# Two attentions: rows of exponentials scaled by VectorE and turned by TensorE as they are, in place of a product with diagonal matrices

## The reference, cut to what matters

```python
scores = jnp.einsum('bhqd,bhkd->bhqk', q, k) * (1.0 / math.sqrt(D))
scores = jnp.where(causal, scores, -jnp.inf)      # L1_ffn only
att = jax.nn.softmax(scores, axis=-1)
y = jnp.einsum('bhqk,bhkd->bhqd', att, v)
y = y.transpose(0, 2, 1, 3).reshape(B, T, C)
return y @ c_proj_w.T
```

## Time and profile before

| | |
|---|---|
| median of three runs | 1833.15 us (1831.13 to 1835.19) |
| profiled execution, its own time | 1833.63 us |
| its span, first to last instruction | 1831.8 us |
| TensorE busy | 1733.0 us, 95% of the span |
| VectorE, ScalarE busy | 623.2 us, 444.4 us |
| mean granted clock of TensorE | 0.985 |

### The profile page before, as it was taken

One profiled execution on the slowest core, in us unless ns is written; L12 is line 12 of the kernel. 1 busy time (PEld: TensorE's weight loads), 2 busy tenths in 40 slices (PEclk: granted clock), 3 DMA queues, 4 the chain that ended last, 5 costly groups with the idle time before them and its releaser, 6 DMA issues.

```text
span 1831.8 us, 27529 instructions
## 1 busy us (share of the span) xinstructions
PE 1733.0 (95%) x12224; PEld 1040.4 (57%) x12224; DVE 623.2 (34%) x1177; ACT 444.4 (24%) x816; POOL 26.8 (1%) x35
## 2 busy tenths in 40 slices
PE   7999999999999999799999988887999999999998
PEld 4675445754476555577654433334675645768664
DVE  4415994049962211543210000002412422133231
ACT  0014883047831110433110000003411010131110
POOL 0000000000000000000000000000001000000000
PEclk9999999999999999899999999999999899999999
DMA  9205986149747877304579999999362164301661
GB/s 379 109 31 171 210 260 243 52 118 218 242 159 282 328 302 303 114 1 155 207 310 387 427 429 429 427 428 428 130 251 103 68 244 193 132 27 52 259 240 64
DMA packets 80750, 408.28 MB, mean 223 GB/s; under 512 B 9768, under 2 KB 50241, under 8 KB 58993
## 3 DMA queue, kind: packets, MB, share of 16 engines
q1 hardware_dynamic: 76112, 402.41, 58.1%
q10 hardware_dynamic: 4512, 4.03, 0.7%
HBM read 400.85 MB, written 5.51 MB: 222 GB/s over the span
## 4 chain that ended last, share of the span: by engine, by line
PE 80%; DMA 13%; DVE 4%; issue 1%; ACT 1%; SPq 0%; POOL 0%; DVEq 0%; ACTq 0%
PE banks L114 78%; DMA weight_ring<-in_L_ffn_c_fc_dram 8%; PE banks L117 2%; DMA weight_ring<-in_L_ffn_c_proj_e_dram 2%; DMA weight_ring<-in_L_gnn_W_in_dram 2%; DVE weight_ring L120 1%; DMA gate_queries<-in_L_gnn_query_rep_dram 1%; DMA node_parts<-gate_node_parts 1%; DVE stat L266 1%; DMA gate_rows<-node_parts 0%; DVE xn_tok L125 0%; DMA ident<-in_c_ident_dram 0%; SPq L154 0%; DVE xT L137 0%; ACT weight_ring L148 0%
## 5 line engine op out<-in xcount | busy, mean ns | idle before, releaser
L114 PE MATMUL banks<-weight_ring,xT 128*128 128x384 f32 x864 | 293.2, 491 | 1.5 <-DVE rgat_xr L137 1.5
L120 DVE TENSOR_TENSOR weight_ring<-weight_ring,gate_queries 128x1024 f32<-128x1024 f32 x192 | 222.7, 1221 | 18.9 <-ACT weight_ring L148 11.3
L114 PEld LDWEIGHTS banks<-weight_ring,xT 128*128 128x128 f32 x864 | 162.6, 191 | 109.0 <-issue 8.7
L148 ACT ACTIVATE weight_ring<-banks 128x1024 f32<-128x1024 f32 x192 | 191.0, 1024 | 44.0 <-PE banks L114 40.8
L114 PE MATMUL banks<-xT,weight_ring 128*128 128x256 f32 x792 | 178.2, 379 | 3.2 <-ACT x_tok L151 3.2
L114 PEld LDWEIGHTS banks<-xT,weight_ring 128*128 128x128 f32 x792 | 149.8, 190 | 27.4 <-issue 3.6
L114 PE MATMUL banks<-weight_ring,r_xd 128*32 128x384 f32 (+1 forms) x2304 | 142.7, 406 | 0.0
L114 PE MATMUL banks<-weight_ring,moe_xdT 128*64 128x384 f32 x720 | 122.0, 489 | 21.4 <-DMA weight_ring<-in_L_ffn_c_fc_dram 20.4
L114 PEld LDWEIGHTS banks<-weight_ring,r_xd 128*32 128x32 f32 x2304 | 76.7, 110 | 63.2 <-issue 54.9
L114 PE MATMUL banks<-gate_rows,selrow 96*128 96x512 bf16 x384 | 107.4, 381 | 2.9 <-ACT weight_ring L148 1.8
L114 PE MATMUL banks<-weight_ring,selrow 128*32 128x256 f32 x1536 | 102.0, 385 | 2.9 <-DVE weight_ring L120 2.7
(11 more groups left out here) (370 smaller groups left out, 1842.7 us busy)
## 6 DMA issues: line engine op xcount, KB each, us to landing
weight_ring<-in_L_ffn_c_fc_dram SPq DMA_DIRECT2D x30, 2304.0 KB, 23.1
weight_ring<-in_L_ffn_c_proj_e_dram SPq DMA_DIRECT2D x21, 2304.0 KB, 28.3
gate_queries<-in_L_gnn_query_rep_dram SPq DMA_DIRECT2D x48, 512.0 KB, 4.6
weight_slot_heads<-in_L_ffn_c_proj_e_dram SPq DMA_DIRECT2D x9, 2304.0 KB, 28.8
weight_ring<-in_L_ffn_w_gate_dram SPq DMA_DIRECT2D x8, 2304.0 KB, 9.8
weight_ring<-in_L_ffn_w_up_dram SPq DMA_DIRECT2D x8, 2304.0 KB, 8.9
weight_ring<-in_L_ffn_w_down_dram SPq DMA_DIRECT2D x8, 2304.0 KB, 9.6
weight_ring<-in_L_ffn_w_dram SPq DMA_DIRECT2D x16, 1152.0 KB, 7.6
```

The costliest lines, as they stand in the source:

```text
L114: return self.e.matmul(out, lhsT, rhs, start=start, stop=stop)
L120: return self.e.tensor_tensor(out, a, b, op)
L148: return self.e.activation(out, a, f, **kw)
```

## The change

VectorE no longer makes diagonal matrices. `diagonals(f)` becomes `normed_rows(f)`: it multiplies each block of rows in `Pm` by the column of inverse sums, in place. TensorE turns the blocks with its transpose, by the identity. The wait for pair f - 3 goes, and so do the two buffers for diagonals. The semaphore of the new name would be one more, so the one for the overflow test's turned column (`worst_ps`) is given up for another key of `slots_ps`.

```diff
         def worst_turn_pe(pe, B):
             pe.wait_ge(*at("worst", B["stage"]))
-            pe.tr(PS[0:1, 4, 0:P], stat[:, 52:53]).then_inc(*mark("worst_ps", B["stage"]))
+            pe.tr(PS[0:1, 4, 0:P], stat[:, 52:53]).then_inc(*mark("slots_ps", (B["stage"], "worst")))
...
         def overflow_dve_flag(v, B):
             s = B["stage"]
-            v.wait_ge(*at("worst_ps", s))
+            v.wait_ge(*at("slots_ps", (s, "worst")))
...
             def turn(h):
-                pe.wait_ge(*at("head_diag", (key, h // 2)))
+                pe.wait_ge(*at("head_normed", (key, h // 2)))
...
                         if k * P < keys_of(c, causal):
-                            t = pe.mm(PS[:, h % 2, n:n + P], Pm[:, h, c, k * P:(k + 1) * P], dg[:, h % 6, c, :], True, True)
+                            t = pe.tr(PS[:, h % 2, n:n + P], Pm[:, h, c, k * P:(k + 1) * P])
                             n += P
...
-            def diagonals(f):
+            def normed_rows(f):
                 sums = stat[:, 32 + 4 * f:36 + 4 * f]
                 v.wait_ge(*at("head_exp", (key, 2 * f + 1)))
-                if f >= LEAD:
-                    v.wait_ge(*at("head_turned", (key, 2 * (f - LEAD) + 1)))
                 v.then(v.rec(sums, sums))
                 for h in (2 * f, 2 * f + 1):
                     for c in range(TC):
-                        t = v.ts(dg[:, h % 6, c, :], ident[:], head_sum_of(h)[:, c:c + 1], ALU.mult)
-                t.then_inc(*mark("head_diag", (key, f)))
+                        row = Pm[:, h, c, 0:keys_of(c, causal is not None)]
+                        t = v.ts(row, row, head_sum_of(h)[:, c:c + 1], ALU.mult)
+                t.then_inc(*mark("head_normed", (key, f)))
...
-                dga = sb("att_diag", [P, 6, TC, P], F32, st)
...
-                dg3 = sb("at3_diag", [P, 6, TC, P], F32, st)
```

More of the change, by code:

```diff
@@ L2146, in head_sum_of, with heads_pe @@
             return stat[:, 32 + TC * h:32 + TC * (h + 1)]
-        def heads_pe(pe, key, units, qT_, kT_, v_, Pm, PT, dg, causal):
+        def heads_pe(pe, key, units, qT_, kT_, v_, Pm, PT, causal):
             def scores(f):
@@ L2247, in heads_act, with heads_dve @@
             weighed(PAIRS - 1)
-        def heads_dve(v, key, units, dsts, Pm, PT, dg, causal):
+        def heads_dve(v, key, units, dsts, Pm, PT, causal):
             def largest(h):
@@ L2271, in diagonals @@
                     for c in range(TC):
-                        t = v.ts(dg[:, h % 6, c, :], ident[:], head_sum_of(h)[:, c:c + 1], ALU.mult)
-                t.then_inc(*mark("head_diag", (key, f)))
+                        row = Pm[:, h, c, 0:keys_of(c, causal is not None)]
+                        t = v.ts(row, row, head_sum_of(h)[:, c:c + 1], ALU.mult)
+                t.then_inc(*mark("head_normed", (key, f)))
             largest(0)
             largest(1)
-            diagonals(0)
+            normed_rows(0)
             for h in range(2, 2 * LEAD):
                 largest(h)
-            diagonals(1)
+            normed_rows(1)
             qkv_copies(v, key, units, dsts, (2,), "dve", 1.0)
@@ L2287, in heads_dve @@
                 if f + LEAD - 1 < PAIRS:
-                    diagonals(f + LEAD - 1)
+                    normed_rows(f + LEAD - 1)
         def cb_bank(e):
@@ L2511, in L1_ffn_pe @@
             queries_pe(pe, "L1_ffn", QKV1)
-            heads_pe(pe, "L1_ffn", QKV1, qTa, kTa, va, Pma, PTa, dga, True)
+            heads_pe(pe, "L1_ffn", QKV1, qTa, kTa, va, Pma, PTa, True)
             pe.wait_ge(*at("rows", ("L1_ffn_y", 1)))
@@ L2625, in L1_ffn_dve @@
             qkv_copies(v, "L1_ffn", QKV1, (qTa, kTa), (0, 1), "dve", 1.0 / math.sqrt(HD))
-            heads_dve(v, "L1_ffn", QKV1, (qTa, kTa, va), Pma, PTa, dga, causal)
+            heads_dve(v, "L1_ffn", QKV1, (qTa, kTa, va), Pma, PTa, causal)
             norm_dve(v, "L1_ffn_2", as_tok(xn_tok[:]), acc_tok, 1e-5, ready=lambda c: at("unit_free", "c_proj"))
@@ L3378, in L3_ffn_pe @@
             queries_pe(pe, "L3_ffn", QKV3)
-            heads_pe(pe, "L3_ffn", QKV3, qT3, kT3, v3, Pm3, PT3, dg3, False)
+            heads_pe(pe, "L3_ffn", QKV3, qT3, kT3, v3, Pm3, PT3, False)
             pe.wait_ge(*at("rows", ("L3_ffn_y", 1)))
@@ L3429, in L3_ffn_dve @@
             qkv_copies(v, "L3_ffn", QKV3, (qT3, kT3), (0, 1), "dve", -1.0 / math.sqrt(HD))
-            heads_dve(v, "L3_ffn", QKV3, (qT3, kT3, v3), Pm3, PT3, dg3, None)
+            heads_dve(v, "L3_ffn", QKV3, (qT3, kT3, v3), Pm3, PT3, None)
             norm_dve(v, "L3_ffn_2", as_tok(xn_tok[:]), acc_tok, 1e-6, center=False,
```

## The result

The changed kernel takes 1827.45 us (median of 20 runs, 1823.63 to 1833.58); the kernel before, beside it, 1833.79 us (20 runs, 1826.27 to 1843.11). The ratio is 0.997, with a 95% interval of 0.9958 to 0.9981: about 6.3 us faster by the medians, where the interval stands for 3.5 to 7.7 us. The profiled execution of the changed kernel took 1825.44 us (span 1823.6).

What follows compares the result with a forecast made beforehand. The prediction took TensorE to bound the kernel, with VectorE and ScalarE setting the pace once in L1_ffn. Gains of 0.47 us (L3_ffn) and 0.20 (L1_ffn), 0.67 in all, took 1833.15 us to 1832.5; range 1829.1 to 1836.5.

Steps and rivals of the forecast that it cites:

- What bounds the kernel now: Whole kernel: TensorE, busy 95% of the span; VectorE and ScalarE set the pace once, in L1_ffn's attention.
- small signs: Attentions: multiplications of 280 and 350 ns, no VectorE pause before head 10's maximum, longer TensorE wait for head 6's copy.
- Step 2: VectorE's scaling in place: 0.12 us more per pair in L1_ffn, 0.24 in L3_ffn, leaving L1_ffn a 0.20 us gain.
- Step 1: TensorE's turns in both attentions: transposes 0.0025 us closer, plus bunch starts; 0.47 us off L3_ffn, 0.40 off L1_ffn.
- entries: Starts of turn bunches in both attentions: second start after 0.169 us instead of 0.212, taken as 0.045 us gained each.
- cover: Both attentions: slack hiding VectorE's longer scaling; a 2.2 us margin in L3_ffn, thin in L1_ffn.
- Step 3: VectorE's dropped wait for pair f - 3 and the overflow test's other counter: worth 0.
- The sum: Both attentions: L3_ffn 0.47 plus L1_ffn 0.20, 0.67 us less in all, giving 1832.5 us.
- A: Attentions: nothing comes off, spacing stays 0.1117 us or VectorE takes the gain; 1833.2 us, chance 0.10.
- B: Attentions: transposes count less for the clock, TensorE falls to 1.2 GHz; 1837.6 us, chance 0.08.
- C: Turns in both attentions: each transpose takes a quarter of the time, 14.1 us off; 1819 us, chance 0.02.
- same: Whole kernel: time not distinguishable from no change, within 0.2% or 3.7 us; chance 0.84.

Runs made afterwards that it cites:

- e1: The changed kernel with the turn again an ordinary product by the identity, scaling in place kept; 1834.16 us, ratio 1.0004.
- e2: The kernel before with turns as transposes, diagonals still built but unused, so no division by the sums; 2264.57 us (one run, with the overflow branch).
- e4: The changed kernel with ScalarE copying turned head 2f + 2 between the exponentials of heads 2f + 6 and 2f + 7; 1826.06 us, ratio 0.9958.
- e6: The changed kernel with the same edit also in L1_gnn's edge attention; 1827.67 us, ratio 0.9973.
- e5: e4 with GpSimd scaling query block 0 of every head and VectorE only block 1; 1830.27 us, ratio 0.9974.
- e7: The changed kernel with diagonals and the ordinary product back in L1_ffn's attention alone; 1829.93 us, ratio 0.9991.
- e8: e4 with VectorE scaling pair f + 2 between the two maxima of pair f + 3; 1826.35 us, ratio 0.9965.

## Why the prediction was wrong

**What bounds the kernel now: right.** TensorE without a wait in L3_ffn and one place of L1_ffn where the others set the pace: what came off TensorE showed in the time. What was missing was the pace of the others: in the kernel before, a lap of L1_ffn took TensorE 3.20 us (from the turns at 862.14 to those at 865.34) and VectorE 2.57 of work (from the scaling at 863.57 to that at 866.14, and the next). A lap of TensorE that falls by more than 0.63 us meets VectorE; it fell by 0.72, and VectorE's rose by 0.14.

All the small signs named for Step 2 came true: scalings of 280 and 350 ns, VectorE's pause ahead of head 10's maximum gone, TensorE's wait for the copy of head 6 longer (1.05 us for 0.21). They said nothing on the time, because the large term stood in the other step.

**Step 1 failed; it is the step that made the forecast wrong.** It took the 72 and 96 records of the earlier trace rows for as many turns and compared a record of a product (0.1117 us) with a record of a transpose (0.1092 us). Both spacings are right, and so are the entries: 0.272 + 0.169 + 4 x 0.109 = 0.88 us is a bunch of L1_ffn to the hundredth, and with 6 in place of 4 it is 1.10 us for L3_ffn's 1.09. Only the count was wrong. A turn cost 2 x 0.1117 = 0.223 us and costs 0.109. That is 0.114 us for each of 84 turns, 9.6 us, where the step had 168 x 0.0025 = 0.42. The rows and the code held the answer: a turn that the code issues 36 times standing at x72, and the x16 of the transposes in the earlier trace rows where the code issues 16. A count of the loop against the count of the row would have shown it.

**Step 2: the durations right, the cover wrong.** The scalings take 280 and 349 ns, four of them 1.01 us in L1_ffn and 1.14 in L3_ffn, as forecast from the earlier trace rows (0.88 + 0.12 and + 0.24). In L3_ffn the margin of 2.2 us ahead of the last pair was to hide it. It does with two passes (e1), but with one pass the same work costs 0.53 us (after against e2). In L1_ffn the forecast let it take 0.20 us (a gain of 0.20 in place of 0.40), and 0.26 came; the size was near, but by another path, since VectorE had been given a TensorE that hardly got faster. From one scaling to the next VectorE needs 2.71 us in L1_ffn and 3.05 in L3_ffn, and goes through them without a pause:

```profile
1608.34 1.14 DVE L124 TENSOR_SCALAR at_P<-at_P,stat 128x256 f32<-128x256 f32 x4
1611.39 1.14 DVE L124 TENSOR_SCALAR at_P<-at_P,stat 128x256 f32<-128x256 f32 x4
1614.45 1.14 DVE L124 TENSOR_SCALAR at_P<-at_P,stat 128x256 f32<-128x256 f32 x4
```

TensorE alone would need 0.80 + 0.86 + 0.80 = 2.46 us for a lap of L1_ffn with turns, scores and weighing (spacing of their starts), and 1.02 + 1.07 + 1.01 = 3.10 us for one of L3_ffn. So VectorE binds in L1_ffn, as the laps of e4 show; in L3_ffn the two are level, and the pair without scores behind them (TensorE 2.0 us) runs into what VectorE and ScalarE still have to do, which is the wait of 0.98 us.

**Step 3: right.** The dropped wait and the other counter's name are worth nothing that shows: e1 has both of them changed, and its attentions last what they did before.

**The sum.** Right terms would have been 9.6 us plus 10 entries at 0.045, 10.0 us off TensorE, of which the new waits take 3.3: 6.7, against the 6.5 measured in the attentions. The size of those waits could not have been read off a row; VectorE's lap of 2.7 us could.

**Rivals.** A did not happen. B did not either: the granted clock stayed at its upper level, 2.4 GHz, through both attentions of the changed kernel (length, busy times, clock, DMA share, GB/s; against the last window of the earlier trace rows):

```profile
858.90:873.30 14.40, 12.26 (x110) 8.37 (x108) 11.74 (x51) 9.66 (x35) 0.00 (x0) 1.00 0.44 164
1604.80:1621.50 16.70, 15.33 (x121) 10.14 (x119) 13.33 (x33) 10.54 (x35) 0.00 (x0) 1.00 0.21 72
```

The Trainium skill's sentence behind B (TensorE: Matmul & The Clock Gate, Part 4, PE-mode transpose) is not borne out by these windows. At most eight transposes stand in a row in them, between scores and weighing products; that this is the reason, no run shows. C was nearest in kind, and I gave it 0.02. I set it aside because sixteen transposes stood 0.1092 us apart; but a record is not a product. Per turn the transpose is 0.223 / 0.109 = 2.04 times as fast. The Trainium skill's four times for fp32 (same page, Terms; it does not say against what) pointed the right way, and is twice what this kernel shows. Where a rule and a row stood that far apart, the row's count deserved a second look.

**The chances.** 0.84 for "same" rested on an effect of 0.04%. That the median came out lower by more than the 3.7 us I could tell apart needed a term outside all my bounds; it was the second pass.

## What to carry to other kernels

Before a row's duration is multiplied, count the instruction in the code and in the row: an ordinary fp32 product stands twice, a transpose once, and a product by an identity or a diagonal, where only a turned copy is wanted, pays both passes. What that gives back is bounded by the next engine's lap, so lay the laps of all engines side by side (here 2.7 and 3.05 us on VectorE) and look at what stands ahead of each copy in the queue of ScalarE. Where another engine's lap is nearly as long and the edit lengthens it, as in L1_gnn, the same edit is worth nothing.

## What the runs showed of the hardware

- An fp32 product of 128x128 by 128 columns: two records, 0.1117 us apart (36 products as 72 records, 48 as 96), weight loads of 192 ns. A transpose of the same shape: one record, 0.109 us to the next, weight loads of 141 ns.
- GpSimd's scaling in place took about 1000 ns for 128x256 fp32 and 702 ns for 128x128, against VectorE's 349 and 280 ns; while it ran, VectorE's 128x256 took 405 ns (L1_ffn) to 460 ns (L3_ffn, up to 570).
- The half-rate stretches of the clock (each costs 1.7 us) move from execution to execution. From L3_ffn's residual to the end the same code took 198.7 us (e6), 200.4 (before, e1) and 202.1 (after, e4, e5, e7, e8), with 0, 1.7 and 3.4 us lost to them in the layer behind the attention. That alone spreads single runs by some microseconds, while the attention stretches repeat to 0.01 us: a change of a few microseconds is better read from its own stretch of the trace than from the median.
